# Head-wise attention of a two-layer block on one core: scores in the V banks, both sums together, and the Q,K projection first

## What is computed

```python
q, k, v = (l2norm(q), l2norm(k), l2norm(v))     # 16 heads; q, k: 16 channels, v: 64
sim = jnp.einsum('bhid,bhjd->bhij', q, k)       # 32 queries by 32 keys, per sequence and head
attn = jnp.square(jax.nn.relu(sim))
out = jnp.einsum('bhij,bhjd->bhid', attn, v)
out = tanh_norm(out)                            # tanh(|out|) * out / |out| per head
return out @ Wout                               # added to x
```

## Time and profile before

| | us |
|---|---|
| median of three runs | 3063.7 (3063.64 to 3067.32) |
| the profiled execution | 3066.01 |
| its span in the trace | 3064.2 |
| second phase in it | about 548 to 806 of the span |

### The profile page before, as it was taken

How to read it: one execution, slowest core, us unless ns; L and a number is a source line. 1 busy time by engine, 2 the same in 40 slices (tenths; PEclk the granted TensorE clock), 3 DMA queues, 4 the chain that set the end, 5 groups by cost and what they waited for, 6 DMA issues and landing times. The chain is left out here.

```text
span 3064.2 us, 80212 instructions
## 1 busy us (share of the span) xinstructions
PE 2600.4 (85%) x29948; PEld 1980.1 (65%) x29949; DVE 2088.2 (68%) x5002; ACT 1473.0 (48%) x4043; POOL 618.3 (20%) x809
## 2 busy tenths in 40 slices
PE   6699999799779999999969999958477777779993
PEld 3488887355568888888847777743143333669993
DVE  6588887576448888888827777765479999632222
ACT  3555554355125555555617777722477765013330
POOL 3355553111000000000002222210222221012224
PEclk8899999899879999999989999979689999769996
DMA  3122221000400000000001111102000001351113
GB/s 94 50 62 67 62 66 34 36 1 0 172 2 3 3 2 2 2 2 2 3 25 32 31 31 31 31 29 117 0 1 1 1 1 56 130 204 38 36 36 93
DMA packets 69020, 121.72 MB, mean 40 GB/s; under 512 B 10176, under 2 KB 51360, under 8 KB 64224
## 3 DMA queue, kind: packets, MB, share of 16 engines
q1 hardware_dynamic: 65424, 109.70, 11.0%
q0 software_dynamic: 3408, 9.31, 1.1%
HBM read 99.12 MB, written 17.69 MB: 38 GB/s over the span
## 5 line engine op out<-in xcount | busy, mean ns | idle before, releaser
L1322 PE MATMUL s_ps<-s3e_xT,s_down 128*128 128x128 f32 x2048 | 256.1, 279 | 1.4 <-issue 1.4
L1322 PEld LDWEIGHTS s_ps<-s3e_xT,s_down 128*128 128x128 f32 x2048 | 245.0, 194 | 15.9 <-issue 10.3
L1333 PE MATMUL s_ps<-s_up,s3e_gh 128*128 128x256 f32 x1024 | 241.9, 380 | 4.2 <-DVE s3e_gh L1491 2.2
L1333 PEld LDWEIGHTS s_ps<-s_up,s3e_gh 128*128 128x128 f32 x1024 | 185.3, 190 | 26.4 <-issue 3.4
L1381 ACT ACTIVATE s3e_gh<-s_ps 128x512 f32<-128x512 f32 x128 | 76.6, 598 | 235.4 <-PE s_ps L1333 211.2
L1736 ACT ACTIVATE s4b_pr<-s4b_sc,s4b_nm 128x257 f32<-128x257 f32 x256 | 127.7, 503 | 109.1 <-DVE s4b_nm L1784 108.9
L2639 ACT ACTIVATE s6e_hT<-s_ps,s_b 128x128 f32<-128x128 f32 x312 | 84.7, 382 | 187.6 <-PE s_ps L2612 187.6
L2280 DVE SCALAR_TENSOR_TENSOR s5c_fresh<-s_ps,s5c_state 128x1024 f32<-128x1024 f32 x124 | 151.3, 1220 | 11.6 <-PE s_ps L2234 4.7
L1367 ACT ACTIVATE s3e_apart<-s3e_number,s3e_picksT 128x128 f32<-128x128 f32 x512 | 156.1, 388 | 1.6
L2663 DVE TENSOR_TENSOR s6e_y<-s_ps,s_b 128x256 f32<-128x256 f32 x39 | 16.6, 424 | 202.4 <-PE s_ps L2626 202.4
L2612 PEld LDWEIGHTS s_ps<-s6e_xT,s6e_w 128*128 128x128 f32 x1248 | 147.2, 194 | 5.5 <-ACT s6e_xT L2643 3.5
(11 more groups left out here) (429 smaller groups left out, 6350.2 us busy)
## 6 DMA issues: line engine op xcount, KB each, us to landing
s_w<-p_w SPq DMA_DIRECT2D x16, 1024.0 KB, 12.8
s4b_cT<-ctxT SPq DMA_DIRECT2D x64, 192.8 KB, 2.4
s1b_cx<-ctx SPq DMA_DIRECT2D x64, 192.0 KB, 2.7
s1b_cT<-ctxT SPq DMA_DIRECT2D x64, 192.0 KB, 3.0
s_results<-s6e_y SPq DMA_DIRECT2D x39, 128.0 KB
s_down<-p_down SPq DMA_DIRECT2D x1, 4096.0 KB, 22.6
s_up<-p_up SPq DMA_DIRECT2D x1, 4096.0 KB, 31.9
s_silu_z<-s5p_sz SPq DMA_DIRECT2D x4, 1024.0 KB, 4.5
```

The costliest lines, as they stand in the source:

```text
L1322: mm = pe.matmul(banks[:, H_BANK + i % 2, tok(e)], lhsT=down[:, k, i * CH + e, :], rhs=xT[:, c.u, k, :], start=k == 0, stop=k == KT - 1)
L1333: mm = pe.matmul(banks[:, Y_BANK, 0:D], lhsT=gh[:, o.u, e, :], rhs=up[:, e, :], start=e == 0, stop=e == NE - 1)
```

## The change

In the second phase alone:

- Scores go into the first half of banks 2 and 3 (those of V), so they wait for V's copy of their tile (`vv_ready`) instead of for `at` and `s_on` of the tile before.
- PE begins a step with the first call of the Q,K projection, then scores, then the second call. The output transposes `out_transposed(0)` follow, the wait for `at`, the first call of V, `out_transposed(1)`, the second call, both halves of the sums, and the other half of V.
- ACT copies the first transposed half ahead of the root for Q and K; its square of V moves from behind `s_qkT` to behind `s_xT`.
- DVE reduces `s_so` ahead of its copy of V; the reduce and floor of V's norm move from before `s_on` to behind it.

The diff, cut to its core:

```diff
                 def score_inputs():
                     pe.wait_ge(qb_ready, t.b + 1)
-                    after(pe, at_ready, t.b)
-                    after(pe, on_ready, t.b)
+                    pe.wait_ge(vv_ready, t.b + 1)
...
-                                mm = pe.matmul(banks[keys, O_BANK + r, D + k * P:D + (k + 1) * P], lhsT=qkT[rows, t.u, KT + k, keys], rhs=qb[rows, t.u, k, :, keys],
+                                mm = pe.matmul(banks[keys, V_BANK + r, tok(k)], lhsT=qkT[rows, t.u, KT + k, keys], rhs=qb[rows, t.u, k, :, keys],
...
-                if c:
-                    pe.wait_ge(xT_ready, c.b + 1)
-                    after(pe, vv_ready, c.b)
-                    project(1, V_BANK, 0)
                 if t:
                     score_inputs()
                 if c:
-                    project(1, V_BANK, 1)
+                    pe.wait_ge(xT_ready, c.b + 1)
+                    after(pe, x_done, c.b - 2)
+                    after(pe, qk_ready, c.b)
+                    project(0, QK_BANK, 0)
                 if t:
                     score()
                 if c:
-                    after(pe, x_done, c.b - 2)
-                    after(pe, qk_ready, c.b)
-                    project(0, QK_BANK, 0)
                     project(0, QK_BANK, 1).then_inc(qk_proj, 1)
-                if t:
-                    sum_inputs()
-                if c:
-                    project(2, V_BANK + 1, 0)
-                if t:
-                    sums(0)
                 if o:
                     out_transposed(0)
+                if t:
+                    pe.wait_ge(at_ready, t.b + 1)
                 if c:
-                    project(2, V_BANK + 1, 1).then_inc(v_proj, 1)
+                    after(pe, vv_ready, c.b)
+                    project(1, V_BANK, 0)
                 if o:
                     out_transposed(1)
                 if t:
+                    after(pe, on_ready, t.b)
+                if c:
+                    project(1, V_BANK, 1)
+                if t:
+                    sums(0)
                     sums(1).then_inc(o_ready, 1)
+                if c:
+                    project(2, V_BANK + 1, 0)
+                    project(2, V_BANK + 1, 1).then_inc(v_proj, 1)
...
+                if t:
+                    dve.wait_ge(sqo_ready, t.b + 1)
+                    dve.tensor_reduce(so[:, t.u, :], heads(sqo[:], H), AXX, ALU.add).then_inc(so_ready, 1)
                 if c:
                     dve.wait_ge(v_proj, c.b + 1)
...
-                if c:
-                    dve.wait_ge(sqv_ready, c.b + 1)
-                    link(dve.tensor_reduce(ss[:, c.u, V], heads(sq[:, c.u, 2 * D:QKV], H), AXX, ALU.add))
-                    root_at_least(V, ssv_ready)
```

More of the change, by code:

```diff
@@ L881, in project @@
                     return pe.matmul(banks[:, bank, :], lhsT=xT[:, c.u, k, :], rhs=w[:, k, n * C:(n + 1) * C], start=k == 0, stop=k == KT - 1)
-                def sum_inputs():
-                    pe.wait_ge(at_ready, t.b + 1)
-                    pe.wait_ge(vv_ready, t.b + 1)
                 def sums(k):
@@ L978, in step @@
                     act.activation(sq[:, c.u, 0:2 * D], banks[:, QK_BANK, :], ACT.Square).then_inc(sqk_ready, 1)
+                if o:
+                    out_transposed(0)
+                if c:
                     act.wait_ge(ssk_ready, c.b + 1)
@@ L992, in step @@
                     act.activation(qkT[:, c.u, :, :], heads(banks[:, TR_BANK, :], 2 * KT), ACT.Copy).then_inc(kT_ready, 1)
-                    act.wait_ge(vv_ready, c.b + 1)
-                    act.activation(sq[:, c.u, 2 * D:QKV], vv[:, c.u, :], ACT.Square).then_inc(sqv_ready, 1)
                 if t:
@@ L1003, in step @@
                 if c:
+                    act.wait_ge(vv_ready, c.b + 1)
+                    act.activation(sq[:, c.u, 2 * D:QKV], vv[:, c.u, :], ACT.Square).then_inc(sqv_ready, 1)
                     act.wait_ge(ssv_ready, c.b + 1)
@@ L1032, in step @@
                         hs = slice(r * H // 2, (r + 1) * H // 2)
-                        ins = dve.scalar_tensor_tensor(at[:, t.u, hs, :], banks[:, O_BANK + r, D:2 * D].rearrange("p (h q) -> p h q", q=S), 0.0,
+                        ins = dve.scalar_tensor_tensor(at[:, t.u, hs, :], banks[:, V_BANK + r, 0:D].rearrange("p (h q) -> p h q", q=S), 0.0,
                                                        bc(rn[:, t.u, V][:, hs].unsqueeze(2), P, H // 2, S), ALU.max, ALU.mult)
@@ L1036, in step @@
                     both = at[:, t.u, :, :].rearrange("p (r h) q -> p r (h q)", r=2)
-                    dve.scalar_tensor_tensor(both, banks[:, O_BANK:O_BANK + 2, D:2 * D], 0.0, both, ALU.max, ALU.mult).then_inc(at_ready, 1)
+                    dve.scalar_tensor_tensor(both, banks[:, V_BANK:V_BANK + 2, 0:D], 0.0, both, ALU.max, ALU.mult).then_inc(at_ready, 1)
                 if c:
@@ L1053, in step @@
                     dve.tensor_copy(vv[:, c.u, :], banks[:, V_BANK:V_BANK + 2, :].rearrange("p n c -> p (n c)")).then_inc(vv_ready, 1)
-                if t:
-                    dve.wait_ge(sqo_ready, t.b + 1)
-                    dve.tensor_reduce(so[:, t.u, :], heads(sqo[:], H), AXX, ALU.add).then_inc(so_ready, 1)
-                if c:
-                    dve.wait_ge(sqv_ready, c.b + 1)
-                    link(dve.tensor_reduce(ss[:, c.u, V], heads(sq[:, c.u, 2 * D:QKV], H), AXX, ALU.add))
-                    root_at_least(V, ssv_ready)
                 if t:
@@ L1068, in step @@
                                       bc(fac[:, t.u, :].rearrange("p (b h) -> p b h", b=NB).unsqueeze(3), P, NB, R4, DV), ALU.mult).then_inc(on_ready, 1)
+                if c:
+                    dve.wait_ge(sqv_ready, c.b + 1)
+                    link(dve.tensor_reduce(ss[:, c.u, V], heads(sq[:, c.u, 2 * D:QKV], H), AXX, ALU.add))
+                    root_at_least(V, ssv_ready)
                 if y:
```

1 line of the change is left out of this document (removed).

## The result

The changed kernel takes 3110.3 us (median of four, 3106.9 to 3113.5) against 3064.4 us of the kernel before on the same chip: a ratio of 1.0148, 95% interval 1.0130 to 1.0165. It is slower by 46 us. The forecast was 3103, within 3078 to 3122. The direction, the place and the mechanism were as forecast; of the terms of the sum the clock's was too small, the other two were too high by less, and one cost was missing. The profiled execution has a span of 3108.3 us, 44.1 more than before.

The account below looks back on a forecast made before the run. The prediction took TensorE as the bound, in a loop closing through `s_on`; +28.9 stall, -3.1 fill and drain and +13.5 clock gave +39.3 on 3066.0, or 3103 us against the median, range 3078 to 3122.

Parts of the forecast that it names:

- What bounds the kernel: Second phase: TensorE looks like the bound, one microsecond in fifteen to win; the loop closes through `s_on`, 14.41 us a period.
- Part one and two, the stall: Steps 4 to 16: TensorE stands about 3.0 us before Q,K for the add into X; 13 x 2.22 = +28.9 us.
- The walk: One steady period added up from profile slots, from the first Q,K half to the add's release of TensorE: 16.63 us.
- The second stall, 0.4 us before the first V half: TensorE, after the second Q,K half and output transposes, waits for `at`: a new stall of 0.41 us.
- The move of V's norm: VectorE: reduce (1.26 us) and floor (0.17) of V's norm, free before, now stand between `s_on` and the add.
- The clock: TensorE at half clock during the first Q,K half and scores after the stall: +13.5 us, 0 to +27.
- four steps in five at 1.3: Half clock after the stall in 0.8 of 13 steps, costing 1.3 us each: +13.5 us.
- Fill and drain: Start and end of the second phase: gains of 0.9, 0.9 and 1.3, together -3.1 us (0 to -5).
- The covers: Moved scores, `so` reduce, V's square and root finish before they are needed, so cost nothing; cover for `so` 0.6 us.
- The sum: 28.9 - 3.1 + 13.5 = +39.3 us on the profiled execution of 3066.0, 3103 us as median; chance 0.60.

Follow-up runs that it names:

- both V calls ahead: Kernel before the change, with both calls of V's first half ahead of the wait for `s_on`, which only the scores need: 3052.2 us, ratio 0.9954.
- filled stalls: Changed kernel with six 256-column matmuls, result overwritten, ahead of the first Q,K half in the 13 steps with an add into X: 3083.1 us, ratio 1.0057.
- TensorE's order alone: Changed kernel's TensorE list and score banks, with ScalarE and VectorE keeping the order of the kernel before: 3097.8 us, ratio 1.0110.
- the early add: Changed kernel with the add into X directly behind `s_on`, ahead of the reduce of V's norm: 3067.1 us, ratio 1.0003.
- the scores ahead: Changed kernel with the scores ahead of the first Q,K half and its wait for the add into X: 3088.9 us, ratio 1.0079.

## Why the prediction was right, and where not

- **What bounds the kernel.** Right: the loop closes through `s_on`, and TensorE had a microsecond to win. The run with both V calls ahead won 0.74 a step of it.
- **Part one and two, the stall.** Right in place and releaser, 13 times. The walk gave 16.63 for the period; at full clock the mean is 16.43, and 16.5 in the inner ten. The term was 28.9 us and measures 26.3. Part of the agreement is luck, since errors cancel. From the first V half to the products with `s_wo` 6.02 us pass (668.93 to 674.95) where the walk had 6.36; its slots had been read between waits, and the calls now run back to back. On the other side the walk missed 0.39 us of VectorE's floor beside GpSimd's copies. The prediction counted GpSimd's masks only as a wait of the scores, never as a neighbour of VectorE, though its row had both ends of the copy.
- **The second stall, 0.4 us before the first V half.** In the changed kernel it is nearly absent (one wait, 0.2 us), since the half clock stretches the work ahead of it. With filled stalls and the full clock it is 0.24.
- **The move of V's norm.** Its 1.4 us do stand between `s_on` and the add, as the walk had it. But the prediction didn't ask what the order without the move would take. TensorE's order alone shows it: the norm ahead of `s_on`, with V's copy ahead of `so`, delays `s_on` by 1.1. So VectorE's moves together cost 0.3 to 0.4 us a step between the products and the release, and not 1.4; they weren't run one by one. What helps is to take the add out from behind it.
- **The clock.** Mis-sized: 13.5 us forecast, 22.3 measured. The step that failed is "four steps in five at 1.3". The stalls of 3.0 to 3.35 us were followed by the half clock in all 13 steps. In nine of them it cost 1.15 to 1.4 us between the first Q,K half and the products, close to the 1.3; in the other four it lasted longer and cost 2.2 to 2.4 (periods of 18.8 to 19.0 beside 17.6 to 18.1). The mean by the periods is 1.71 a step. The bounds, 0 to 27, held it. With 22.3 in place of 13.5 the forecast would have been 3112.
- **Fill and drain.** -3.1 forecast. Measured: -4.2 at the start (4.9 less the 0.7 ahead of the phase), where the forecast had -1.8, and -0.5 at the end, where it had -1.3: -4.7. The drain gained less than thought, since the second transposes, which now stand ahead of both sums, still wait for `at`:

```profile
829.53 1.12 PE L902 MATMUL s_ps<-x_ident,s_on 128*128 128x128 f32 x4 [3.11 <-DVE s_at L1035]
830.58 1.96 PE L888 MATMUL s_ps<-s_vv,s_at 32*32 32x64 f32 x128
```

- **The covers.** `so` ahead of V's copy held: `s_no` follows ScalarE's copy of the transposes without a wait (0.49 after its start in the changed kernel). V's square was ready before the reduce wanted it. From `s_no` to tanh, with the table load, pass 1.52 us in the changed kernel (675.64 to 677.16), as in the row that the prediction used.
- **The sum.** 26.3 + 22.3 - 4.7 + 0.9 = 44.8, and less the 0.7 by which the phase starts earlier 44.1, the difference of the two spans. The forecast had +39.3. The clock was 8.8 short; the stall, 2.6 too high, and fill and drain, 1.6 too high, made up for half of that by chance.

The rule that the prediction weighed, that TensorE with short idle times between groups of matmuls swings between its clocks (the Trainium skill, TensorE: Matmul & The Clock Gate, section on psum-queue depth-cycling), is borne out by the changed kernel with its 3.3 us, and not by the kernels with stalls of 0.7 and 1.6 us, whose clock was 1.00 in the steady part, nor by TensorE's order alone, where it was 1.00 from the fourth of the 13 stalls on.

## What to carry to other kernels

Before a matmul group is moved forward in an engine's list, look at every wait that it carries: a wait that was met a microsecond early costs nothing where it stands, and holds up everything when it stands first. Ask then which engine raises it and in what place of its own list; moving one short operation there (an add of 0.4 us) was worth 43 us here. And price a stall of TensorE twice, once for its length and once for the clock that may follow, which a few matmuls put into the stall can test on the chip.

## What the runs showed of the hardware

- A small VectorE operation beside a GpSimd tensor operation can be held until that ends: 16 columns in 0.56 and 0.77 us instead of 0.17, and a multiplication with two inputs in SBUF 0.49 instead of 0.17, while a reciprocal kept its 0.25. The Trainium skill (GPSIMD Engine Reference, its table row on SBUF interfaces) says that GpSimd shares them with VectorE, with contention for instructions of a 2-port mode or with two SBUF inputs. The traces agree for the multiplication. That the floor runs in such a mode no run here shows.
- The length of a stall alone doesn't decide on the clock. In the kernel with the early add 1.3 to 1.7 us cost nothing in any of 13 steps. With the scores ahead, stalls of 1.9 to 2.6 us were followed by the half clock in 12 of 13 steps (mean 0.89); in the changed kernel 3.0 to 3.35 us were in all 13. Yet stalls of 2.8 and 3.1 us in TensorE's order alone went on at 1.00 from the fourth on. What tells these apart was not tried; it stays open.
- TensorE did more work in less time: 13 x 2.6 us of matmuls in its stalls took 22 us from the second phase.
